# Five experts' weights split ahead of time in the self-attention stage, stored in two parts and loaded whole in the expert stage

## The reference

```
w, sel = _route(x, gate_weight, expert_bias)
cw = (one_hot(sel, NUM_EXPERTS) * w[..., None]).sum(1)
y = silu(x @ g.T) * (x @ u.T) @ d.T          # for each expert
out = out + cw_e[:, None] * y
```

## Time and profile before

| | us |
|---|---|
| median of 3 runs | 1485.21 (1482.55 to 1486.15) |
| the profiled execution, its own time | 1482.78 |
| its span, first to last instruction | 1480.7 |
| TensorE busy (matmul) | 1349.8 (91%) |
| DVE busy | 800.2 (54%) |
| ACT busy | 729.6 (49%) |
| GpSimd busy | 577.0 (39%) |
| mean granted TensorE clock | 0.961 of full speed |

### The profile page before, as it was taken

The page is one execution under the profiler, slowest core; times in us unless marked ns, Lnnn a source line. Parts: engine busy times, 40 slices in busy tenths (PEclk is TensorE's granted clock), DMA queues, the critical chain, the costliest instruction groups (busy, mean ns, idle before and its releaser), DMA issues. The chain is left out here.

```text
span 1480.7 us, 22809 instructions
## 1 busy us (share of the span) xinstructions
PE 1349.8 (91%) x7136; PEld 1105.5 (75%) x7136; DVE 800.2 (54%) x1372; ACT 729.6 (49%) x1736; POOL 577.0 (39%) x350
## 2 busy tenths in 40 slices
PE   5998699999999999999985999998889989999991
PEld 4776477878787878787864888887678768787771
DVE  4434366666666666666654444445389843433245
ACT  2444366565656565656543677777321213343330
POOL 2430143323242414141103333334347396327975
PEclk9998799999999999999997999999799999999995
DMA  5785414141515141412041243442633156536767
GB/s 211 250 274 175 175 45 155 51 177 42 184 42 184 42 184 42 184 42 114 1 171 59 82 133 107 135 135 99 230 129 133 71 199 223 184 107 227 246 197 220
DMA packets 78984, 209.79 MB, mean 142 GB/s; under 512 B 5888, under 2 KB 39168, under 8 KB 72960
## 3 DMA queue, kind: packets, MB, share of 16 engines
q1 hardware_dynamic: 69472, 163.78, 32.0%
q0 software_dynamic: 7136, 38.80, 7.9%
q10 hardware_dynamic: 2304, 6.29, 1.1%
HBM read 154.59 MB, written 92.01 MB: 167 GB/s over the span
## 5 line engine op out<-in xcount | busy, mean ns | idle before, releaser
L745 DVE TENSOR_TENSOR probsT_lo<-psTr,probsT_hi 128x512 fp32r<-128x512 f32 x256 | 176.7, 690 | 166.2 <-ACT probsT_hi L698 165.9
L698 ACT CAST probsT_hi<-psTr 128x512 fp32r<-128x512 f32 x256 | 150.2, 587 | 197.0 <-PE psTr L835 193.3
L835 PE MATMUL psTr<-ident,probs 128*128 128x128 f32 x1024 | 153.6, 274 | 12.1 <-DVE probsT_lo L745 6.0
L835 PEld LDWEIGHTS psTr<-ident,probs 128*128 128x128 f32 x1024 | 124.1, 141 | 51.4 <-DVE probsT_lo L745 14.7
L740 DVE TENSOR_REDUCE nmax<-psS 128x1 f32<-128x1024 f32 x128 | 155.5, 1215 | 9.3 <-PE psS L81 8.2
L606 POOL TENSOR_TENSOR w_slots<-ctx_f,w_slots 128x512 fp32r<-128x512 f32 x32 | 41.4, 1294 | 279.4 <-ACT w_slots L657 279.4
L650 ACT ACTIVATE probs<-psS,nmax 128x1024 f32<-128x1024 f32 x128 | 143.7, 1123 | 12.1 <-DVE nmax L740 12.1
L79 PE MATMUL psS<-w_slots 128*128 128x512 f32 x256 | 113.0, 441 | 3.8 <-DMA w_slots<-qe 2.9
L79 PE MATMUL psV<-probsT_hi,w_slots 128*128 128x512 f32 x256 | 114.8, 449 | 0.7
L79 PE MATMUL bank<-w_slots,ao_first_hi 128*128 (+1 forms) x244 | 103.5, 424 | 6.1 <-POOL w_slots L1589 3.0
L1589 POOL TENSOR_TENSOR w_slots<-w_ahead,w_slots 128x3072 fp32r<-128x3072 f32 x15 | 102.2, 6812 | 1.2
(11 more groups left out here) (287 smaller groups left out, 3310.2 us busy)
## 6 DMA issues: line engine op xcount, KB each, us to landing
w_ahead<-w_exp POOLq DMA_DIRECT2D x14, 1536.0 KB, 7.4
qe<-stage SPq DMA_DIRECT2D x16, 1024.0 KB, 6.8
w_slots<-qe SPq DMA_DIRECT2D x16, 1024.0 KB, 5.0
wraw<-w_pairs SPq DMA_DIRECT2D x8, 1792.0 KB, 11.2
early<-xs SPq DMA_DIRECT2D x47, 256.0 KB, 2.7
xs<-h_rows SPq DMA_DIRECT2D x47, 256.0 KB, 2.0
early<-ctx SPq DMA_DIRECT2D x16, 512.0 KB, 11.1
ao<-attn_out SPq DMA_DIRECT2D x32, 256.0 KB, 2.9
```

What stands on the lines that cost most here:

```text
L698: act.copy(PT[k % PTN].hi[:], psT[slot][:]).then_inc(turned_hi, 1)
L745: dve.tensor_tensor(out, psT[slot][:], f32(hi), ALU.subtract).then_inc(turned_free, 1)
L835: last = pe.transpose(psT[slot][:, q * P:(q + 1) * P], src(q), ident[:])
```

## The change

- **Self stage.** GpSimd splits the weights of experts 7, 9, 11, 13 and 15, one expert in each of the token tiles 1 to 5, in three pieces of 128 x 1024. SP loads a piece into the first half of a `w_ahead` chunk; GpSimd copies it into the second half (high part) and subtracts in place (low part); SP stores both to a DRAM array `w_pre`.
- **Expert stage.** For these five experts GpSimd issues two loads of 1536 KB from `w_pre` into the slot. The next expert's subtraction comes behind `whole_ready`, a wait on GpSimd for both loads. The other ten experts are split as before, with the raw load two ahead in their own order.
- **w_o.** Its chunks are loaded in the first four steps of the last pass, the first into a buffer of its own.
- **Fills.** Three in each of cross iterations 1 to 6, none in the self stage.
- The semaphores of the cross loop are cleared by SP in the self stage and given back for later use.

```diff
@@ build_cross, SP
         def iteration(i, first, last):
+            if not (first or last):
+                fill(FILLS * i - FILLS)
             if not last:
-                fill(2 * i)
                 for j in range(2):
                     load_kv(2 * i + 2 + j)
...
-            if not last:
-                fill(2 * i + 1)
+                if not (first or last):
+                    fill(FILLS * i - FILLS + 1 + j)
@@ build_self
-WO_STEPS = (2, 4, 6, 7)
+WO_STEPS = (0, 1, 2, 3)
+PIECES, PIECE = 3, KC * BANK // 2
+PRE_FIRST, PRE_STEP, NPRE = 7, 2, NT - 3
-    wo_raw = keep["ahead"] + [sb("wo_last", [P, KC, BANK])[:]]
+    wo_raw = [sb("wo_first", [P, KC, BANK])[:]] + keep["ahead"]
+    sets = [a.rearrange("p k x -> p (k x)") for a in keep["ahead"]]
+    p_raw, p_high = ([a[:, j * PIECE:(j + 1) * PIECE] for a in sets] for j in range(2))
+    def group(i, v):
+        return 2 * i - 1 + v // HKV
@@ build_self, SP
+        for done in keep["cleared_later"]:
+            sp.sem_clear(done)
         def step(i, v, last):
             u, tt, g, ahead = plan(i, v, last)
-            if isinstance(u, int) and u in WO_STEPS:
-                c = WO_STEPS.index(u)
-                if c == 0:
-                    sp.wait_ge(w_ready, WCH)
+            pre_moves(i, v, last)
+            if last and v in WO_STEPS:
+                c = WO_STEPS.index(v)
+                if c:
+                    sp.wait_ge(p_out[c - 1], 32 * NPRE)
                 sp.dma_start(wo_raw[c], t["w_o"][:, c * KC:(c + 1) * KC, :]).then_inc(wo_in[c], 16)
...
-            if g == 2 and not last and not isinstance(i, int):
-                r = 2 * NT - 4 + 2 * i + v // HKV
-                sp.dma_start(t["xs_r"][r], t["zeros"]).then_inc(keep["fill_in"], 16)
+        def pre_moves(i, v, last):
+            g = v % HKV
+            if g < PIECES and has_before(i, v):
+                m = group(i, v) - 1
+                sp.wait_ge(pre_lo, PIECES * m + g + 1)
+                for part, src in enumerate((p_high[g], p_raw[g])):
+                    sp.dma_start(t["w_pre"][m, part, g], src).then_inc(p_out[g], 16)
+            if g >= 1 and has_group(i, v, last):
+                m = group(i, v)
+                if isinstance(i, int):
+                    if v == HKV + 1:
+                        sp.wait_ge(w_ready, WCH)
+                else:
+                    sp.wait_ge(p_out[g - 1], 32 * m)
+                sp.dma_start(p_raw[g - 1], t["w_exp"][PRE_STEP * m + PRE_FIRST + 1, :, (g - 1) * PIECE:g * PIECE]).then_inc(
+                    p_in[g - 1], 16)
@@ build_self, GpSimd step: between rope_q and norm, and behind norm
+            if g == 3 and has_group(i, v, last):
+                pre_low(group(i, v), 0)
+            if g < 2 and has_before(i, v):
+                pre_low(group(i, v) - 1, g + 1)
             if ahead(1):
                 norm(u + 1, (v + 1) % 2)
+            if g >= 2 and has_group(i, v, last):
+                pre_high(group(i, v), g - 2)
+            if g == 0 and has_before(i, v):
+                pre_high(group(i, v) - 1, 2)
@@ build_moe, GpSimd
+        def whole_load(e):
+            for part in range(2):
+                pool.dma_start(f32(slot(e)[part]).rearrange("p (s c) -> p s c", s=PIECES),
+                               t["w_pre"][WHOLE.index(e), part].rearrange("s p c -> p s c")).then_inc(whole_in, 16)
+
+        def whole_ready(e):
+            pool.wait_ge(w_ready, e)
+            pool.wait_ge(whole_in, 32 * (WHOLE.index(e) + 1))
+            pool.sem_inc(w_ready, 1)
...
             pool.sem_inc(slot_free, 1)
-            pool.tensor_copy(slot(e)[0], raw[(e + 1) % 2]).then_inc(pool_hi, 1)
-            pool.wait_ge(pool_hi, e)
-            expert_low(e)
-            if e + 2 < NE:
-                expert_load(e + 2)
+            if e in WHOLE:
+                whole_load(e)
+                continue
+            pool.tensor_copy(slot(e)[0], raw[j % 2]).then_inc(pool_hi, 1)
+            if e - 1 in WHOLE:
+                whole_ready(e - 1)
+            pool.wait_ge(pool_hi, j + 1)
+            expert_low(e, j)
+            if j + 2 < len(SPLIT):
+                expert_load(j + 2)
+        whole_ready(NE - 1)
```

More of the change, by code:

```diff
@@ L476 @@
 FIRST = 4
+FILLS = 3
 def build_cross(nc, ctx, sem, t, keep):
@@ L944, in build_self @@
     tab = sb("rope_s_tab", [P, 2, 3, DH // 2])
-    wo_raw = keep["ahead"] + [sb("wo_last", [P, KC, BANK])[:]]
+    wo_raw = [sb("wo_first", [P, KC, BANK])[:]] + keep["ahead"]
+    sets = [a.rearrange("p k x -> p (k x)") for a in keep["ahead"]]
+    p_raw, p_high = ([a[:, j * PIECE:(j + 1) * PIECE] for a in sets] for j in range(2))
+    p_in, p_out = keep["pre_in"], keep["pre_out"]
+    pre_seen, pre_hi, pre_lo = sem("pre_seen"), sem("pre_hi"), sem("pre_lo")
     WO = [Shared(ws, c * WSZ, (KC, D)) for c in range(HQ // 2 // KC)]
@@ L1002, in plan, with has_group, has_before, i_last @@
         return GI * i + v, 2 * i + v // HKV, v % HKV, ahead
+    def group(i, v):
+        return 2 * i - 1 + v // HKV
+    def has_group(i, v, last):
+        return not last and not (isinstance(i, int) and v < HKV)
+    def has_before(i, v):
+        return not (isinstance(i, int) and i == 0) and not (i_last(i) and v >= HKV)
+    def i_last(i):
+        return isinstance(i, int) and i == NT // 2 - 1
     def turns(eng, step):
@@ L1096, in step, with pre_high, pre_low @@
                 pool.tensor_copy(AS.hi, a_first).then_inc(wo_hi, 1)
+        def pre_high(m, j):
+            pool.wait_ge(p_in[j], 16 * m + 16)
+            pool.sem_inc(pre_seen, 1)
+            pool.tensor_copy(p_high[j].bitcast(F32R), p_raw[j]).then_inc(pre_hi, 1)
+        def pre_low(m, j):
+            pool.wait_ge(pre_hi, PIECES * m + j + 1)
+            pool.tensor_tensor(p_raw[j].bitcast(F32R), p_raw[j], p_high[j], ALU.subtract).then_inc(pre_lo, 1)
         def wo_high(c):
@@ L1368 @@
 NBLK = NE * NT + DUMMY
-assert NBLK // NT == 2 * NT - 2 + 2 * (NT // 2 - 2)
+assert NBLK // NT == FILLS * (NT - 2)
 XR, YR, HR = 4, 3, 3
@@ L1372 @@
 ON_WAY = 3
+WHOLE = tuple(PRE_FIRST + PRE_STEP * m for m in range(NPRE))
+SPLIT = tuple(e for e in range(1, NE) if e not in WHOLE)
+assert WHOLE[-1] == NE - 1 and PIECES * PIECE == 2 * KC * I + NIT * D
 C_BIAS, C_TRI, C_TRIG, C_DIAG = 0, NE, NE + NE * NE, NE + NE * NE + NG * NG
@@ L1493, in build_moe @@
     sh_hi, sh_lo, e0_hi, e0_lo = sem("sh_hi"), sem("sh_lo"), sem("e0_hi"), sem("e0_lo")
-    pool_hi, w_ready = sem("pool_hi"), sem("w_ready")
+    pool_hi, w_ready, whole_in = sem("pool_hi"), sem("w_ready"), sem("whole_in")
     a_mm, silu_made, prod_made, hid_hi, hid_lo = (
@@ L1586, in slot, with expert_low, expert_load @@
             return WS[:, at:at + wcol], WS[:, at + wcol:at + 2 * wcol]
[L1588 to L1593, removed]
+        def expert_low(e, j):
+            pool.tensor_tensor(slot(e)[1], raw[j % 2], f32(slot(e)[0]), ALU.subtract).then_inc(w_ready, 1)
+        def expert_load(j):
+            pool.wait_ge(w_ready, SPLIT[j - 2] + 1 if j >= 2 else 1)
+            pool.dma_start(raw[j % 2], t["w_exp"][SPLIT[j] + 1]).then_inc(pool_in[j % 2], 16)
+        def whole_load(e):
[6 more added lines that the diff above has]
+            pool.sem_inc(w_ready, 1)
         pool.sem_inc(a_lo, 1)
@@ L1615, in _ @@
         pool.sem_inc(w_ready, 1)
-        expert_load(2)
+        expert_load(1)
         for e in range(1, NE):
@@ L1619, in _ @@
                 pool.wait_ge(table_made, 2)
[L1620 to L1623, removed]
+            if e in SPLIT:
+                j = SPLIT.index(e)
+                if j == 0:
+                    pool.wait_ge(raw_in[0], 32)
+                else:
+                    pool.wait_ge(pool_in[j % 2], 16 * ((j + 1) // 2))
+            if e == WHOLE[0]:
+                for j in range(PIECES):
+                    pool.wait_ge(keep["pre_out"][j], 32 * NPRE)
             if e == 1:
@@ L2138, in build @@
         for name, n in (("ht_in", 2), ("wqkv_in", HQ // REP + 1), ("wo_in", W_AHEAD + 1), ("a_in", 2),
-                        ("ao_out", 2)):
+                        ("ao_out", 2), ("pre_in", 3), ("pre_out", 3)):
             keep[name] = [sem(f"{name}{j}") for j in range(n)]
@@ L2147, in build, with sem_second @@
                 build_queries(nc, ctx, sem_first, t, keep)
+            keep["cleared_later"] = []
+            second_sems = ExitStack()
+            def sem_second(name):
+                keep["cleared_later"].append(second_sems.enter_context(nc.semaphore(name)))
+                return keep["cleared_later"][-1]
             with ExitStack() as ctx:
-                build_cross(nc, ctx, sem, t, keep)
+                build_cross(nc, ctx, sem_second, t, keep)
         first.close()
@@ L2157, in build @@
             build_self(nc, ctx, sem, t, keep)
+        second_sems.close()
         with ExitStack() as ctx:
@@ L2242 @@
     t["xs"] = nc.dram_tensor("xs", (NBLK, P, D), F32).ap()
+    t["w_pre"] = nc.dram_tensor("w_pre", (NPRE, 2, PIECES, P, PIECE), F32).ap()
```

## The result

The changed kernel takes 1491.4 us (median of 7 runs, 1487.24 to 1495.38), the kernel before 1484.5 us in the same series. The ratio is 1.0049, 95% interval 1.0033 to 1.0065: slower by 0.5%, 7 us. The profiled execution after took 1487.24 us, span 1485.2: 4.5 us over the span before. It is the fastest of its seven, so its trace shows rather too little of the loss than too much.

A forecast was written before the change was run, and what follows sets the result against it. GpSimd was taken as the bound late in the expert stage, the gathers standing behind expert 15. Terms 0 + 0 + 11.4 on the profiled 1482.8 us gave 1494; with 2.4 to the median, 1496.5, range 1482 to 1508.

The forecast's parts named there:

- One of its signs: Expert stage: GpSimd idle some 6 us or more ahead of subtractions of experts 10, 12 and 14, released by a DMA.
- Self stage, fills, w_o: Added self-stage work, moved fills and moved w_o loads are covered by idle time: zero us; fills 0 to +2.
- The chain of landings: Expert stage, GpSimd: landing, subtraction and issues in series, 6.0 us of data per 1536 KB; expert 15 ready 11.4 us later.
- TensorE's waits: Expert stage: TensorE waits about 6 us at tile 35, less at tiles 36, 40 and 42.
- The gathers move with expert 15: End of kernel: gathers start later with expert 15, first near 1435 us, as do tile 42 and the dummies; overlap unchanged.
- Rival 1: Expert stage: whole experts land in 10.1 us, expert 15 ready 5.7 us earlier, kernel time 1479.5 us; chance 0.12.
- the tiles' traffic: Expert stage, DMA engines: 116 GB/s of tile traffic can wait a little beside a single load, less beside back-to-back loads.

The follow-up runs named there:

- e4: The changed kernel with GpSimd's subtraction and next raw load ahead of the wait for the whole expert: 1485.1 us, 1.0006 of the kernel before.
- e1: The changed kernel up to the end of the self stage, but the expert stage splits all fifteen experts as before: 1485.4 us, 1.0002 of the kernel before.
- e5: The changed kernel with the eight gathers of the first choice issued before GpSimd waits for expert 15: 1487.4 us, 1.0020 of the kernel before.
- e3: The changed kernel loading only the high part of each whole expert, 1536 KB instead of 3072: 1477.9 us, 0.9958 of the kernel before.
- e12: The changed kernel with SP's row loads and stores ahead of the wait for the last store in tiles 1 to 36: 1495.0 us, 1.0053.
- e9: e4 with SP's row loads and stores ahead of the wait for the last store in tiles 1 to 36: 1476.0 us, 0.9928 of the kernel before.

## Why the prediction was right

The sign, the place and the mechanism were right, and the time was in the range; the size was too high, +11.4 where 7 were measured and 4.5 show in the profile. One of its signs can't be read: it wanted GpSimd's waits released by a DMA, and the profile names none there; that they were landings follows from the program and from e4. By its steps:

- **Self stage, fills, w_o: zero.** Right (e1). The gap behind the subtraction was as worked out. These rows answer to the earlier trace rows: 0.51 us are left before the norm, where I had 0.3, and 0.27 before the next L1107 (L1069 before).

```profile
904.39 1.04 POOL L1147 CAST w_ahead<-w_ahead 128x1024 fp32r<-128x1024 f32 x1
905.70 1.29 POOL L1107 TENSOR_TENSOR q_rope<-q_terms 128x512 f32<-128x512 f32 x1 [0.27 <-DVE q_terms L1240]
906.95 2.40 POOL L1151 TENSOR_TENSOR w_ahead<-w_ahead 128x1024 fp32r<-128x1024 f32 x1
909.86 1.05 POOL L1111 TENSOR_TENSOR sprobs<-sprobs,srinv 128x512 f32<-128x512 f32 x1 [0.51 <-DVE srinv L1262]
```

- **The chain of landings: right in form, too long in size.** Ready times forecast and measured: expert 11 at 1391.4 and 1388.5, 13 at 1412.6 and 1407.5, 15 at 1433.8 and 1426.9. The whole experts took 14.3, 17.4, 12.3 and 12.6 us from the issue (forecast 12 to 14, and 18 or more for expert 11). The mis-sized term is the landing, 2.2 to 2.3 us fixed and 6.0 us per load of 1536 KB. From the end of a subtraction to the next landing there were 18.8 us for three loads (forecast 20.2) and 12.3 and 12.5 for two (forecast 14.3 each): 5.2 us less in three links. Both parts were too long. These two stretches follow the subtraction that ended at 1395.3 us, with the columns of the earlier trace rows:

```profile
1395.30:1396.50 1.20, 1.08 (x5) 0.92 (x6) 0.00 (x0) 0.44 (x1) 1.20 (x2) 1.00 0.00 0
1396.50:1407.50 11.00, 11.00 (x59) 9.08 (x58) 3.20 (x7) 4.32 (x10) 3.00 (x2) 1.00 0.99 368
```

  The DMA engines stood still for 1.2 us, where I had 2.3, and were then full for 11.0 us until expert 13 had landed, at most 5.5 us per load where I had 6.0. I had sized the data time by 333 GB/s at 0.98 busy as if that were the most. Here they moved 368, and 403 between 1375 and 1386 us, when TensorE stood still for part of the time. The first landing came 1.4 us before the forecast, 1362.9, since the slot was free 1.25 us earlier, and three subtractions took 0.1 us less each. 11.4 - 5.2 - 1.4 - 0.3 = 4.5, as the profile shows.
- **TensorE's waits: right, the size in part by luck.** Tile 35 waited 6.2 us (forecast 6). But expert 11 was ready 2.9 us before the forecast and TensorE wanted it at 1382.3, 3.4 us before: two errors that cancelled. Tile 42 waited 2.3 us, tile 36 0.3 us, tile 40 nothing that shows.
- **The gathers move with expert 15 and their own length stays: right.** The first gather came at 1428.4 (forecast near 1435). The length to the gathers grew by 5.6 us, the length from them on is 56.8 in both. e5 shows that a part of it, 4 us, is this order alone.
- **Rival 1 (the loads are quick enough):** it did not happen with the wait where it is; with half the bytes (e3) it did, at 0.9958. In the Trainium skill, "DMA: Bandwidth & Descriptors", section "Anatomy of one DMA", the formula comes to 9.2 us for 3072 KB, an estimate that takes the two loads as one; the four waits of the trace have 12.3 at the least, beside the tiles' traffic, and no single load of `w_pre` landed under 7.5 us. The prediction had held 333 GB/s against this formula; the 403 GB/s above show that the engines can do more.
- **What the prediction didn't see:** the second limit behind the first, SP's order. It had put the tiles' traffic down as something that can wait a little. The order cost nothing while GpSimd's chain was the bound (e12), and 9 us once it wasn't (e4 against e9).

## What to carry to other kernels

Before work is swapped for a transfer on an in-order engine, look at what is put behind the wait for the landing: here 6.8 us of subtraction and the issue of the next transfer made each landing a link of a serial chain, and the same bytes with the wait behind them cost nothing. Then ask who else uses the DMA engines at that time and in which order a queue waits: a load of data needed later should not stand behind the wait for a store. One fix alone may show nothing; e4 gave parity and the row order gave nothing in either kernel, and together they gave 0.7%.

## What the runs showed of the hardware that was not expected

- Six operations a tile more on GpSimd and 64 GB/s more on the DMA engines left TensorE's steady self stage alone: 202.1 busy us of 204 in both.
- A store of 256 KB from SP, which landed in 2.0 us at the median from 1300 to 1345 us (before; an expert was loading for 7 of these 45 us), took 6.1 us between 1370 and 1395 us, in the kernel before already. The row loads went from 2.7 to 5.3 us there, and to 7.8 us in the changed kernel. How the engines share between the queues wasn't tried apart.
- The zero fills land in 16.8 us at the median with three of them in an iteration, against 10.7, and TensorE's cross loop didn't change.
- The issue of a load of 384 pieces of 4 KB took 0.76 us on GpSimd, against 0.56 for 128 rows of 12 KB.
- After its longest waits TensorE worked at half the clock: 0.50 for 3.3 us of work behind the wait of 6.2 us (changed kernel), and 0.50 from 1437 to 1442 us in e5, about the end of the wait of 11.3 us.
- The 16 DMA engines moved 403 GB/s over 11 us (1375 to 1386 us, changed kernel), against 333 in the fullest stretch that the prediction had read.
